# Non-local attention in one core: the high-half value matmuls placed ahead of the scores in two of eight steps, and the spread peak of g read first

## The reference

```python
g     = (einsum('bchw,oc->bhwo', x, w_g) + b_g).reshape(B, N, Ci)          # Ci = 64
theta = (einsum('bchw,oc->bhwo', x, w_theta) + b_theta).reshape(B, N, Ci)
phi   = (einsum('bchw,oc->bohw', x, w_phi) + b_phi[:, None, None]).reshape(B, Ci, N)
att   = softmax(einsum('bnc,bcm->bnm', theta, phi), axis=-1)
y     = einsum('bnm,bmc->bnc', att, g)
out   = einsum('bhwc,oc->bohw', y, w_out) + b_out
inv   = bn_gamma / sqrt(bn_var + 1e-5)
return x + out * inv + (bn_beta - bn_mean * inv)
```

## Time and profile before

| | us |
|---|---|
| median of 3 runs (211.96 to 212.52) | 212.36 |
| the profiled execution | 212.18 |
| its span in the trace | 210.4 |
| TensorE busy (94%) | 198.5 |
| VectorE busy (85%) | 178.4 |
| GpSimd busy (72%) | 152.4 |
| ScalarE busy (65%) | 136.8 |

### The profile page before, as it was taken

The page is one execution under the profiler, slowest core; times in us unless marked ns, Lnnn a source line. Parts: engine busy times, 40 slices in busy tenths (PEclk is TensorE's granted clock), DMA queues, the critical chain, the costliest instruction groups (busy, mean ns, idle before and its releaser), DMA issues.

```text
span 210.4 us, 3966 instructions
## 1 busy us (share of the span) xinstructions
PE 198.5 (94%) x1100; PEld 130.9 (62%) x1100; DVE 178.4 (85%) x291; ACT 136.8 (65%) x245; POOL 152.4 (72%) x127
## 2 busy tenths in 40 slices
PE   7996989999999998999999999999999998999993
PEld 6585856586565856577555955667565854566542
DVE  0789899978998799978999599978999699989871
ACT  2776866758575847767577666756578575658721
POOL 2448898699669998699778998699887964774400
PEclk9999999999999999999999999999999999999999
DMA  5215967999999998899959995899977997786111
GB/s 156 88 60 154 212 126 155 229 215 168 230 106 247 229 183 167 165 249 232 189 129 259 220 200 133 190 252 216 153 160 167 224 170 166 134 108 114 50 37 66
DMA packets 59500, 35.28 MB, mean 168 GB/s; under 512 B 50400, under 2 KB 50912, under 8 KB 59488
## 3 DMA queue, kind: packets, MB, share of 16 engines
q1 hardware_dynamic: 59200, 35.01, 81.2%
q10 hardware_dynamic: 288, 0.14, 0.2%
HBM read 8.36 MB, written 4.23 MB: 60 GB/s over the span
## 4 chain that ended last, share of the span: by engine, by line
PE 58%; DVE 15%; ACT 12%; issue 10%; DMA 2%; ACTq 1%; DVEq 0%
PE ps_scores L721 17%; PE ps_y L733 11%; PE ps_flip L786 9%; ACT probs L544 8%; PE ps_misc L705 6%; DVE neg_max L586 6%; DVE pt_lo L686 5%; PE ps_y L740 5%; ACT pt_hi L532 4%; PE ps_misc L747 3%; PE ps_misc L811 3%; DVE y_norm L603 2%; PE ps_scores L759 2%; DMA w_tp<-w_tp_t_dram 2%; PE ps_flip L705 1%
## 5 line engine op out<-in xcount | busy, mean ns | idle before, releaser
L544 ACT ACTIVATE probs<-ps_scores,neg_max 128x1024 f32<-128x1024 f32 x64 | 71.7, 1120 | 32.3 <-DVE neg_max L591 23.4
L586 DVE TENSOR_REDUCE neg_max<-ps_scores 128x1 f32<-128x1024 f32 x64 | 77.8, 1216 | 0.9 <-PE ps_scores L721 0.9
L686 DVE SCALAR_TENSOR_TENSOR pt_lo<-ps_flip,pt_hi 128x512 f16<-128x512 f32 x84 | 54.0, 685 | 15.8 <-ACT pt_hi L532 15.6
L532 ACT ACTIVATE pt_hi<-ps_flip 128x512 f16<-128x512 f32 x84 | 45.7, 596 | 20.4 <-PE ps_flip L786 20.1
L721 PE MATMUL ps_scores<-phi_hh,theta_hl 128*128 128x512 f32 x128 | 45.8, 439 | 5.2 <-ACT probs L544 4.8
L426 POOL TENSOR_TENSOR p_lo<-probs,p_hi 128x1024 f16<-128x1024 f32 x22 | 47.1, 2141 | 4.3 <-POOL p_hi L422 2.6
L786 PE MATMUL ps_flip<-ident,probs 128*128 128x128 f32 x336 | 45.0, 276 | 1.0 <-ACT probs L544 0.6
L786 PEld LDWEIGHTS ps_flip<-ident,probs 128*128 128x128 f32 x336 | 37.2, 142 | 11.6 <-issue 5.7
L721 PE MATMUL ps_scores<-phi_ll,theta_hl 128*128 128x512 f32 x128 | 40.1, 394 | 0.0
L422 POOL TENSOR_SCALAR p_hi<-probs 128x1024 f16<-128x1024 f32 x22 | 23.6, 1071 | 11.3 <-ACT probs L544 8.3
L721 PEld LDWEIGHTS ps_scores<-phi_hh,theta_hl 128*128 128x128 f32 x128 | 19.3, 190 | 18.9 <-ACT probs L544 17.5
(11 more groups left out here) (80 smaller groups left out, 176.8 us busy)
## 6 DMA issues: line engine op xcount, KB each, us to landing
x_in<-x_in_dram SPq DMA_DIRECT2D x16, 256.0 KB, 3.3
inv_all<-inv_row SPq DMA_DIRECT2D x15, 256.0 KB, 4.1
out_dram<-resid SPq DMA_DIRECT2D x15, 256.0 KB, 2.7
phi_hh<-hi SPq DMA_DIRECT2D x14, 256.0 KB, 5.2
phi_ll<-lo SPq DMA_DIRECT2D x14, 256.0 KB, 5.7
theta_hl<-hi SPq DMA_DIRECT2D x7, 256.0 KB, 4.3
theta_hl<-lo SPq DMA_DIRECT2D x7, 256.0 KB, 5.1
pt_hi<-p_hi SPq DMA_TRANSPOSE x22, 4.5
```

Source lines behind the costliest of these rows:

```text
L532: nc.scalar.activation(pt_hi[ring][:, c * HALF_TILES:(c + 1) * HALF_TILES, slot * P:(slot + 1) * P], ps_flip[c][:, :].rearrange("p (a n) - ...
L544: nc.scalar.activation(probs[k % PROB_RING][:, :], ps_scores[k % 2][:, :], ACT.Exp, bias=neg_max[:, k % STEPS:k % STEPS + 1], accum_out=ro ...
L586: nc.vector.tensor_reduce(out=top, in_=ps_scores[k % 2][:, :], op=ALU.max, axis=AX.X, negate=True).then_inc(row_max_ready if by_dma(it, k) ...
L686: nc.vector.scalar_tensor_tensor(out=pt_lo[ring][where], in0=ps_flip[c][:, :].rearrange("p (a n) -> p a n", n=P), scalar=PROB_SCALE, in1=p ...
```

## The change

Two groups of instructions are moved and none is added or taken away.

On TensorE `sum_high` with its four waits stood behind the scores (and the convolution or projections) of steps 3 and 7. It now stands ahead of the scores in these steps. The last two halves have calls of their own, which stay as they are.

On VectorE the read of the spread peak (L655) stood behind L627 and L631 in step 0. It now is the first operation of step 0, for images 1 to 7. For image 0, where it stands in step 2, nothing changes. The operations that use it keep their place.

```diff
--- before.py
+++ after.py
@@ -580,6 +580,11 @@
                 nc.vector.tensor_reduce(out=g_peak[:, r:r + 1], in_=g_raw[r][:, :, :], op=ALU.max, axis=AX.XY,
                                         apply_absolute_value=True).then_inc(g_peak_ready, 1)
 
+            def read_peak(b, r, spread):
+                dve.wait_ge(g_peak_spread, b + 1)
+                nc.vector.tensor_reduce(out=g_peak_all[:, r:r + 1], in_=spread[:, 0:P], op=ALU.max,
+                                        axis=AX.X).then_inc(g_peak_read, 1)
+
             def row_maximum(it, k):
                 top = neg_max[:, k % STEPS:k % STEPS + 1]
                 dve.wait_ge(scores_ready, tile_at(it, k) + 1)
@@ -615,6 +620,9 @@
 
             def step(it, k):
                 image, j = image_at(it, k), k % MT
+
+                if j == 0 and exists(image, B) and not is_first(image):
+                    read_peak(image, k // MT % 2, ps_misc)
 
                 t = tile_at(it, k - 1)
                 if exists(t, TILES) and ((k - 1) % HALF_TILES == HALF_TILES - 1 or in_last_half(t)):
@@ -650,10 +658,8 @@
 
                 if j == (2 if is_first(image) else 0) and exists(image, B):
                     r = k // MT % 2
-                    dve.wait_ge(g_peak_spread, image + 1)
-                    spread = ps_y if is_first(image) else ps_misc
-                    nc.vector.tensor_reduce(out=g_peak_all[:, r:r + 1], in_=spread[:, 0:P], op=ALU.max,
-                                            axis=AX.X).then_inc(g_peak_read, 1)
+                    if is_first(image):
+                        read_peak(image, r, ps_y)
                     dve.wait_ge(g_peak_read, image + 1)
                     nc.vector.tensor_scalar(out=g_unit[:, r:r + 1], in0=g_peak_all[:, r:r + 1],
                                             scalar1=G_LEAST, scalar2=1.0 / G_TOP,
@@ -787,6 +793,15 @@
                                                        probs[(k - 2) % PROB_RING][:, m * P:(m + 1) * P],
                                                        ident[:, :])
                         last.then_inc(flipped, 1)
+
+                h, quarter = half_at(it, k - 6), (k - 6) % HALF_TILES
+                if quarter == 1 and exists(h, HALVES - 2):
+                    ring, r = ring_of(k - 6), (k - 6) // MT % 2
+                    pe.wait_ge(pt_lo_ready, 2 * flip_at(it, k - 7 + HALF_TILES))
+                    pe.wait_ge(hi_moved[ring], moved_by(it, k - 6))
+                    pe.wait_ge(g_split, image_at(it, k - 6) + 1)
+                    wait(pe, y_scaled, h)
+                    sum_high(ring, r, ps_y, slice(0, BANK), slice(0, BANK))
 
                 t = tile_at(it, k + 1)
                 if exists(t, TILES):
@@ -828,12 +843,6 @@
                 h, quarter = half_at(it, k - 6), (k - 6) % HALF_TILES
                 if exists(h, HALVES - 2):
                     ring, r = ring_of(k - 6), (k - 6) // MT % 2
-                    if quarter == 1:
-                        pe.wait_ge(pt_lo_ready, 2 * flip_at(it, k - 7 + HALF_TILES))
-                        pe.wait_ge(hi_moved[ring], moved_by(it, k - 6))
-                        pe.wait_ge(g_split, image_at(it, k - 6) + 1)
-                        wait(pe, y_scaled, h)
-                        sum_high(ring, r, ps_y, slice(0, BANK), slice(0, BANK))
                     if quarter == 3:
                         pe.wait_ge(lo_moved[ring], moved_by(it, k - 6))
                         sum_low(ring, r, ps_y, slice(0, BANK), slice(0, BANK))
```

## The result

The changed kernel takes 208.72 us (median of 5, 208.51 to 210.12) against 212.36 us (median of 5, 211.90 to 212.77). The ratio is 0.985, with a 95% interval of 0.982 to 0.987: 1.5% faster, 3.6 us. I had forecast 211.7 us with a range down to 210.9. The largest term, the fills in step 3, had the right sign and a quarter of the measured size. The fill in step 7 and the loss in the last image were near, and the read of the spread peak, forecast to cost 0.13 us, gained.

The account below looks back on a forecast made before the run. TensorE, busy 198 of 210 us, was taken to set the pace, so reordering wins only its gaps. The terms -0.69 -0.55 +0.42 +0.13 sum to -0.69 us, a median of 211.7 us, range 210.9 to 212.9.

Parts of the forecast that it names:

- fills in step 3: TensorE, tile 4's scores: the high half fills idle behind the convolution in images 2, 4 and 6, together -0.69 us.
- fill in step 7: TensorE, tile 8's scores: only image 0 has a gap, 0.94 us, which the high half partly fills, -0.55 us.
- loss in the last image: VectorE, image 7: later scores delay pt_lo(58) and the next tile's transposes, with no cover, +0.42 us.
- the read of the spread peak: VectorE, step 0: hidden under L631's wait for GpSimd, 0 in images 1 to 6 and +0.13 us in image 7.
- My bound of 0.05 us for each small gap: TensorE, step 3 of images 1, 3 and 5: gaps from convolution end to scores could add -0.15 us.
- My expected sign: Step 3: tile 2's transposes 0.3 us earlier against their convolution in images 2 and 4, unchanged in 1, 3 and 5.
- The sign that I had named for being wrong: TensorE: a wait for hi_moved ahead of the high half beyond image 0 would show the prediction wrong; no size given.
- Later scores: Steps 3 and 7: scores go back 1.73 us; images 1 to 6 pay nothing, the last image +0.42 us.
- A larger gain: Rival: the last image's VectorE chain has missed slack and small gaps count, -1.3 us, 211.1 us; chance 0.15.
- Fills don't last: Rival: VectorE gives the start of step 5 and takes the gain back, about 212.3 us; chance 0.26.
- Slower: Rival: VectorE becomes the bound in step 0, max(9) and exp(1) 0.53 us late, +0.9, 213.3 us; chance 0.12.

Follow-up runs that it names:

- e9: Kernel before, order untouched, but the exp of tile 2 of images 1 to 7 takes only the first 512 of 1024 columns: 209.41 us in one execution.
- e5: Changed kernel with only the first two of eight high-half matmuls ahead of the scores in steps 3 and 7: 208.66 us, ratio 0.985.
- e8: Kernel before with the high half ahead of the scores in step 7 alone, step 3 and the read as before: 211.77 us, ratio 0.999.
- e1: Changed kernel measured and profiled again, nothing edited: 208.70 us median, ratio 0.985 against the kernel before.
- e2: Changed kernel with only TensorE's move, the read of the spread peak back behind the scaling: 208.94 us, ratio 0.985 against the kernel before.
- e3: Kernel before with only VectorE's read of the spread peak moved, TensorE's order as before: 211.54 us against 212.01, ratio 0.998.

## Why the prediction was wrong, point by point

**Fills in step 3: wrong.** The step that failed is "Images 1, 3, 5 and 7 have no gap there that a row shows, and I count nothing for them". I forecast -0.69 us for all of step 3 and the measured sum is -2.76. The overlap was wrong: I took the end of the convolution's row for the moment at which TensorE is free, and an unmet wait for one that costs only the idle shown. The kernel before lost 0.32 to 0.33 us in each of images 1, 3 and 5, 0.39 in image 6 (0.11 forecast), 0.58 and 0.56 in images 2 and 4 (0.30 and 0.28 forecast) and 0.25 in image 7. In image 1 it is made of 0.21 us of idle that the row doesn't show, as the next work could start 0.86 us after the convolution's start and exp ended 1.02 us after it, and of 0.13 us from there on, where the weight load of the scores stood behind its wait.

e9 shows that it is the wait (5.70 to 5.39 with the order untouched), e5 that two ready matmuls ahead, 0.4 us, hide it. The row that says so was in the same list of waits as rows 2, under PEld. The Trainium skill, "TensorE: Matmul & The Clock Gate", section "Architectural detail: the array is 16× 32×32, not 1× 128×128", says that TensorE's queue can pull weight loads ahead of matmuls in flight. The traces agree (39.27 during the convolution) and show the other side: not past a wait of their own that isn't met (40.62, after 0.88 us of waiting in PEld).

My bound of 0.05 us for each small gap has the same fault: it starts from the modelled end of the convolution. My expected sign, transposes of tile 2 unchanged against their convolution in images 1, 3 and 5, failed for that reason. I also spoke of fifteen places that the diff touches; there are fourteen, seven in step 3 and seven in step 7, and no term hangs on it.

**Fill in step 7: right, size a little small.** Image 0 gave 0.69 us up to tile 0 of image 1, against 0.55. In the changed kernel's first profile the high half started at 28.05 and not at 28.6:

```profile
28.05 1.90 PE L739 MATMUL ps_y<-pt_hi,g_parts 128*128 128x512 f16 x8
29.59 0.81 PE L727 MATMUL ps_scores<-phi_hh,theta_hl 128*128 128x512 f32 x2
...
30.82 1.03 PE L792 MATMUL ps_flip<-ident,probs 128*128 128x128 f32 x8
...
31.93 1.07 ACT L532 ACTIVATE pt_hi<-ps_flip 128x512 f16<-128x512 f32 x2
...
DMA to landing us min/median/max: 5.5/5.5/5.5
```

The hi transpose was issued at 22.0 and landed 5.5 us later this time, at 27.5, so TensorE won 1.22 us at the transposes of tile 6. ScalarE took 0.74 of it (31.93 against 32.67), as it was held by exp(7) until then, which is the limit that I had put. The start that I had forecast was the landing of one execution: in e8 it landed after 6.5 us again, the high half started at 28.61, and image 0 won 0.64 at the transposes of tile 6 and 0.59 up to tile 0 of image 1. So the limit of ScalarE makes both come out near my 0.55. That the gain lives on only through step 3 is what e8 shows. In the other six images the swap wins nothing up to the transposes of tile 6. My reason there, "the scores follow it at once", was read from the PE row again; the PEld row has a wait of 0.66 to 0.68 us in each, and it is the residual behind that keeps the swap at nothing.

The sign that I had named for being wrong, a wait for hi_moved beyond image 0, did show up in the first profile (0.57 us in step 7 of image 2), with the landing of 7.9 us, but not in the PE row of e1. It cost time in that execution and isn't why the forecast failed.

**Later scores: right.** Images 1 to 6 pay nothing. The idle in front of pt_lo(2) is gone and that in front of pt_lo(3) is smaller by 0.39 (image 2 of the changed kernel, against the two rows of image 1 in the earlier trace rows):

```profile
67.39 1.29 DVE L692 SCALAR_TENSOR_TENSOR pt_lo<-ps_flip,pt_hi 128x512 f16<-128x512 f32 x2
...
70.58 1.29 DVE L692 SCALAR_TENSOR_TENSOR pt_lo<-ps_flip,pt_hi 128x512 f16<-128x512 f32 x2 [0.58 <-ACT pt_hi L532]
```

In the last image I forecast a loss of 0.42 us and measured 0.33. Row maximum of tile 4, low half of tile 2 and transposes of tile 3 in e1:

```profile
183.41 1.23 DVE L591 TENSOR_REDUCE neg_max<-ps_scores 128x1 f32<-128x1024 f32 x1 [0.95 <-PE ps_scores L727]
...
184.82 1.28 DVE L692 SCALAR_TENSOR_TENSOR pt_lo<-ps_flip,pt_hi 128x512 f16<-128x512 f32 x2
...
185.65 1.16 PE L792 MATMUL ps_flip<-ident,probs 128*128 128x128 f32 x8 [0.47 <-DVE pt_lo L692]
```

pt_lo(58) starts 1.61 us after its transposes (183.21), where it was 1.27. I had added up to 1.7.

**The read: small, and with the wrong sign.** Priced at 0 in images 1 to 6 and +0.13 in image 7. With the high half moved it is worth 0.2 us (e2 against e1), within what can be told. Without it, 0.47 (e3). I had written that exp(1) comes 0.15 earlier and taken no gain from it. In e3 it comes 0.33 us earlier (image 2), and images 2 and 4 waited for just that chain. The wait at L631 was read rightly, though it fell only to between 0.17 and 0.74 us in e1, where I had expected 0.15 to 0.3. And I hadn't seen the reverse of it: an instruction that is put later to meet p_hi's end can miss it and meet p_lo, and the scaling then took 1.99 us.

**The rivals.** "A larger gain" was the right one, for a reason that isn't the one I gave. "Fills don't last" needs VectorE to gate step 5, and 3.52 to 3.54 us from the transposes of tile 2 to those of tile 3 in images 1 to 6, before and in e1, says that it doesn't. "Slower" needs it to be late in step 0, and steps 4 to 1 became 0.35 us shorter.

**What stays open.** The 0.13 us behind the wait comes with a weight load that couldn't go ahead. How much of it is the load and how much the start of matmuls after an idle isn't separated. Nor do I have a profile of a second execution near 210 us, so that these executions are all the stall of L639 is not shown, and that the late DMA brought the stall about rests on one trace.

## What to carry to other kernels

Where TensorE waits for another engine, read the PEld row as well as PE. Here a wait that ended together with the work ahead of it left no idle in the PE row and cost 0.14 us; one that ended up to 0.2 us later still left almost none and cost 0.3 us. Some ready work belongs between them. Two matmuls were enough in step 3, and they keep the delayed work's own readers nearly on time; image 0's wait of 0.94 us in step 7 needed all eight. A hidden wait is worth something only where nothing later holds the engine anyhow: six of the fourteen, in step 7, were worth nothing. To price such a place, compare start to start between two groups that don't change, with and without the wait.

## What was not expected of the hardware

The prediction counted with VectorE being held by GpSimd at L631, but not with how much depends on the form. A scaling of 128x2 elements is held by a GpSimd instruction that runs beside it, and one of 128x1 isn't: 0.660 us in the mean in the kernel before and up to 1.99, against 0.150 to 0.154 in every group of the one-column form. Where the wide form took longer than 0.18 us it ended within 0.04 us of GpSimd's p_hi or, in one case, p_lo. Splitting seven such instructions in two took 0.76 us off the kernel before.
